# Two attentions of a two-layer network: strips gathered by DMAs of 48, 16 and 32 partitions, and the second attention's scores and sums taken by key blocks

## What is computed

```python
# first attention ("ratio")
q, k, v = split(LN(x) @ w_qkv + b_qkv)
dot     = q @ k.T                                     # per head, 512 x 512
scores  = dot * dot / (|q|^2 + |k|^2 - 2 * dot + 1e-6) # causal
x       = x + softmax(scores) @ v @ w_out + b_out
# second attention ("zeroed")
q, k, v = split(LN(x).reshape(heads) @ Wqkv + bqkv)
att     = (q @ k.T / 4) * tril(ones, k=-1)            # zeroed, not left out
x       = x + softmax(att) @ v @ Wr + br
```

## Time and profile before

| | |
|---|---|
| median of 3 runs | 2644.44 us |
| lowest, highest | 2637.9, 2645.82 us |
| the profiled execution | 2632.14 us |
| its span in the trace | 2630.4 us |
| TensorE matmul, busy | 2454.3 us (93%) |
| TensorE weight loads | 1750.0 us (67%) |
| VectorE | 2083.8 us (79%) |
| ScalarE | 1996.4 us (76%) |
| GpSimd | 1787.9 us (68%) |
| DMA, SP's and ScalarE's queues | 106176 packets and 175.82 MB; 3840 packets and 1.58 MB |

### The profile page before, as it was taken

One profiled execution on the slowest core, in us unless ns is written; L12 is line 12 of the kernel. 1 busy time (PEld: TensorE's weight loads), 2 busy tenths in 40 slices (PEclk: granted clock), 3 DMA queues, 4 the chain that ended last, 5 costly groups with the idle time before them and its releaser, 6 DMA issues. The chain is left out here.

```text
span 2630.4 us, 71983 instructions
## 1 busy us (share of the span) xinstructions
PE 2454.3 (93%) x25252; PEld 1750.0 (67%) x25252; DVE 2083.8 (79%) x6697; ACT 1996.4 (76%) x3679; POOL 1787.9 (68%) x3824
## 2 busy tenths in 40 slices
PE   5999999999999999999879989999999999989998
PEld 3677676667767666777423347767776777668887
DVE  5898898889889889988664578878888888846665
ACT  4999899999999999999524347677677666667776
POOL 4778778778877877887361137777777777756555
PEclk8999999999999999999989999999999999999999
DMA  4344244334334433433100146556655655400011
GB/s 119 65 74 81 55 73 85 72 61 83 72 58 79 85 71 61 77 69 63 37 6 1 37 74 111 99 101 98 106 101 95 105 104 94 64 1 32 25 33 41
DMA packets 110375, 182.00 MB, mean 69 GB/s; under 512 B 27008, under 2 KB 96384, under 8 KB 97920
## 3 DMA queue, kind: packets, MB, share of 16 engines
q1 hardware_dynamic: 106176, 175.82, 35.8%
q10 hardware_dynamic: 3840, 1.58, 0.4%
HBM read 116.25 MB, written 60.29 MB: 67 GB/s over the span
## 5 line engine op out<-in xcount | busy, mean ns | idle before, releaser
L921 POOL TENSOR_SCALAR ratio_scores<-ratio_scores,ratio_max_cols 128x512 f32<-128x512 f32 (+3 forms) x1024 | 539.3, 535 | 169.7 <-DVE ratio_max_cols L799 169.5
L205 PE MATMUL bank<-ratio_k_stack,ratio_q_stack 102*128 102x512 bf16 (+7 forms) x2048 | 508.7, 303 | 42.3 <-DVE ratio_max_cols L799 21.3
L1491 DVE CUSTOM_DVE_ANT_0 zeroed_unused<-bank,zeroed_drop 128x512 bf16<-128x512 f32 (+3 forms) x1024 | 439.7, 485 | 107.4 <-PE bank L205 107.2
L799 DVE CUSTOM_DVE_ANT_0 ratio_scores<-bank,ratio_scores 128x512 f32<-128x512 f32 (+3 forms) x1024 | 472.5, 490 | 22.2
L1373 ACT ACTIVATE arena<-bank 128x512 f32<-128x512 f32 x640 | 370.2, 593 | 151.0 <-PE bank L1266 149.6
L789 DVE TENSOR_TENSOR ratio_scores<-bank,ratio_inverse 128x512 f32<-128x512 f32 x640 | 435.6, 681 | 13.5 <-ACT ratio_inverse L648 6.5
L655 ACT ACTIVATE ratio_prob<-bank 128x512 f32<-128x512 f32 x640 | 378.6, 592 | 81.8 <-PE bank L554 80.9
L644 ACT ACTIVATE ratio_inverse<-bank 128x512 f32<-128x512 f32 x640 | 382.6, 598 | 13.4 <-PE bank L208 13.2
L554 PE MATMUL bank<-const_f_sb,ratio_scores 128*128 128x128 f32 x2560 | 386.5, 273 | 1.2 <-ACT ratio_prob L655 1.0
L648 ACT ACTIVATE ratio_inverse<-ratio_inverse 128x1024 f32<-128x1024 f32 x320 | 338.6, 1058 | 10.1
L1625 POOL TENSOR_SCALAR_AFFINE_SELECT arena<-arena 128x256 f32<-128x256 f32 (+1 forms) x640 | 228.0, 362 | 165.7 <-ACT arena L1373 161.2
(11 more groups left out here) (218 smaller groups left out, 4872.0 us busy)
## 6 DMA issues: line engine op xcount, KB each, us to landing
ratio_q_stack<-ratio_parts_q SPq DMA_DIRECT2D x186, 128.0 KB
ratio_k_stack<-ratio_parts_k SPq DMA_DIRECT2D x186, 128.0 KB
zeroed_q_stack<-zeroed_parts_q SPq DMA_DIRECT2D x186, 128.0 KB, 4.5
zeroed_k_stack<-zeroed_parts_k SPq DMA_DIRECT2D x186, 128.0 KB, 7.5
ratio_parts_q<-arena SPq DMA_DIRECT2D x96, 128.0 KB
ratio_parts_k<-arena SPq DMA_DIRECT2D x96, 128.0 KB
zeroed_parts_q<-shared_parts SPq DMA_DIRECT2D x96, 128.0 KB
zeroed_parts_k<-shared_parts SPq DMA_DIRECT2D x96, 128.0 KB
```

The lines of the kernel that those rows point to most:

```text
L205: i = e.matmul(bank[:, off:off + w], qs[0:rows, s, hh, ib * P:(ib + 1) * P], ks[0:rows, s, hh, 0:w], start=(k == 0), stop=mask is None, sk ...
L799: i = e.tensor_tensor_reduce(seg, dot_banks[n % 2][:, at], seg, 1.0, 0.0, ALU.mult, ALU.max, mx[:, pair % M_BUFS, c:c + 1])
L921: i = e.tensor_scalar(seg, seg, -1.0, mx[:, pair % M_BUFS, c:c + 1], ALU.mult, ALU.add)
L1491: i = e.tensor_tensor_reduce(unused[:, n % 2, at], bank[:, at], drop[:, L - (ib + 1) * P:L], 1.0, 0.0, ALU.add, ALU.max, mx[:, pair % FOLD ...
```

## The change

The k parts are stored in DRAM in reverse (part 2 first), the q parts as before. Then strips 0 to 2, strip 3 and strips 4 and 5 of both stacks are each a run of parts that lie next to each other in DRAM, and one DMA of 48, 16 or 32 partitions copies a run: six DMAs for a half instead of twelve. The six products of parts that a matmul sums are the same, in another order. The bytes are the same.

In the second attention `shift` no longer goes by query blocks. A unit now holds key blocks (`KEY_UNITS`: key block `jb = 3 - ib` with the queries from `jb` on, which has as many columns as query block `ib` had), one matmul for each segment. `attend_keys` sums in the order of key blocks 0, then 1 and 3, then 2, one matmul per head and key block over all queries from that block on, accumulating in the bank. `keep` picks the diagonal blocks at their new places: the first block of each segment.

The diff, without the two counts of semaphores in the first attention's `denoms` and the second's `dots`, which change in the same way as `gathered`:

```diff
-Q_PARTS = (0, 0, 1, 0, 2, 1)
-K_PARTS = (0, 1, 0, 2, 0, 1)
+STORED = ((0, 1, 2), (2, 1, 0))
+RUNS = ((0, 3, (0, 0)), (3, 1, (0, 2)), (4, 2, (0, 1)))
+GATHERS = 2 * len(RUNS)
+
+def gather_run(e, side, run, stack, dst, heads, stored):
+    strip, n, first = run
+    return e.dma_start(stack[strip * HD:(strip + n) * HD, dst, heads, :],
+                       stored[first[side]:first[side] + n, :, heads, :].rearrange("k d h t -> (k d) h t"))
...
-        gathered = lambda half: (s[f"gathered{half % 2}"], 16 * (14 * (half // 2 + 1) - 2 * (half % 2 == 0)))
+        gathered = lambda half: (s[f"gathered{half % 2}"], 16 * ((GATHERS + 2) * (half // 2 + 1) - 2 * (half % 2 == 0)))
...
-            for strip, part in enumerate((Q_PARTS, K_PARTS)[side]):
-                q.e.dma_start((qs, ks)[side][strip * HD:(strip + 1) * HD, st, heads, :],
-                              part_dram[side][st][part][:, heads, :]).then_inc(sem, 16)
+            for run in RUNS:
+                gather_run(q.e, side, run, (qs, ks)[side], st, heads, part_dram[side][st]).then_inc(sem, 16)
...
-                    e.dma_start(part_dram[side][half % 2][part].rearrange("d h t -> h d t"),
+                    e.dma_start(part_dram[side][half % 2][STORED[side][part]].rearrange("d h t -> h d t"),
                                 parts[:, side, part, :]).then_inc(s[f"parts_{sides[side]}"], 16)
...
+KEY_UNITS = [[(h, 3 - ib, off) for h, ib, off in segs] for segs in UNITS]
+WHERE_KEYS = {(h, jb): (u, off) for u, segs in enumerate(KEY_UNITS) for h, jb, off in segs}
+KEY_ATTEND = tuple(tuple(3 - ib for ib in blocks) for blocks in ATTEND)
...
-                first = True
-                for h, ib, off in UNITS[u]:
-                    wd, hh = (ib + 1) * P, (g % 2) * GROUP + h
-                    for jb in range(ib + 1):
-                        i = e.matmul(bank[:, off + jb * P:off + (jb + 1) * P], ks[0:STACK + FOLD_ROWS, st, hh, jb * P:(jb + 1) * P],
-                                     qs[0:STACK + FOLD_ROWS, st, hh, ib * P:(ib + 1) * P], start=first, stop=True, skip_group_check=True)
-                        first = False
+                for k, (h, jb, off) in enumerate(KEY_UNITS[u]):
+                    hh = (g % 2) * GROUP + h
+                    i = e.matmul(bank[:, off:off + L - jb * P], ks[0:STACK + FOLD_ROWS, st, hh, jb * P:(jb + 1) * P],
+                                 qs[0:STACK + FOLD_ROWS, st, hh, jb * P:L], start=(k == 0), stop=True, skip_group_check=True)
                 i.then_inc(s["shifted"])
+
+            def attend_keys(g, part):
+                vs, base = (g // 2) % STACKS, g * N_UNITS
+                for jb in KEY_ATTEND[part]:
+                    for h in range(GROUP):
+                        u, off = WHERE_KEYS[h, jb]
+                        i = e.matmul(o_bank[32 * h:32 * h + 32, jb * P:L], values_ones[:, vs, jb, (g % 2) * GROUP + h, :],
+                                     prob[:, (base + u) % FOLD_PROBS, off:off + L - jb * P],
+                                     start=(jb == 0), stop=(part == len(KEY_ATTEND) - 1), skip_group_check=True)
+                return i
...
-                    attend(e, g, part, o_bank, values_ones, prob, FOLD_PROBS, STACKS).then_inc(s["attended"])
+                    attend_keys(g, part).then_inc(s["attended"])
...
-                units = UNITS[n % N_UNITS]
+                units = KEY_UNITS[n % N_UNITS]
                 to = prob[:, n % FOLD_PROBS, :].rearrange("p (k t) -> p k t", k=T)
-                diagonal = to[:, 1::2, :] if len({ib for _, ib, _ in units}) < len(units) else to[:, T - len(units):T, :]
+                diagonal = to[:, 0:units[-1][2] // P + 1:max(units[-1][2] // P, 1), :]
```

More of the change, by code:

```diff
@@ L210, in product, with attend @@
     return i
-def attend(e, g, part, o_bank, values_ones, prob, bufs=PROB_BUFS, stacks=2):
-    vs, base = (g // 2) % stacks, g * N_UNITS
+def attend(e, g, part, o_bank, values_ones, prob):
+    vs, base = (g // 2) % 2, g * N_UNITS
     for ib in ATTEND[part]:
@@ L221, in attend @@
                              values_ones[:, vs, jb, (g % 2) * GROUP + h, :],
-                             prob[:, (base + u) % bufs, off + jb * P:off + (jb + 1) * P],
+                             prob[:, (base + u) % PROB_BUFS, off + jb * P:off + (jb + 1) * P],
                              start=(jb == 0), stop=(jb == ib), skip_group_check=True)
@@ L536, in denoms @@
             def denoms(n):
-                q.wait_ge(s["gathered_first"], 16 * 14)
+                q.wait_ge(s["gathered_first"], 16 * (GATHERS + 2))
                 if n >= N_UNITS:
@@ L1205, in zeroed_attention @@
         sides = "qk"
-        gathered = lambda half: (s[f"gathered{half % STACKS}"], 16 * 12 * (half // STACKS + 1))
+        gathered = lambda half: (s[f"gathered{half % STACKS}"], 16 * GATHERS * (half // STACKS + 1))
         folded = lambda pair: (s[f"m_folded{pair % 4}"], 16 * (pair // 4 + 1))
@@ L1250, in dots @@
             def dots(n):
-                q.wait_ge(s["gathered_first"], 16 * 12)
+                q.wait_ge(s["gathered_first"], 16 * GATHERS)
                 if n >= N_UNITS:
@@ L1682, in gather @@
                 q.wait_ge(s["shifted"], (half + 1 - STACKS) * HALF_UNITS)
-                for stack, side, order in ((qs, 0, Q_PARTS), (ks, 1, K_PARTS)):
-                    for strip, part in enumerate(order):
-                        e.dma_start(stack[strip * HD:(strip + 1) * HD, dst, heads, :],
-                                    part_dram[side][st][part][:, heads, :]).then_inc(sem, 16)
+                for stack, side in ((qs, 0), (ks, 1)):
+                    for run in RUNS:
+                        gather_run(e, side, run, stack, dst, heads, part_dram[side][st]).then_inc(sem, 16)
             for half in range(2, halves):
@@ L2141, in send_parts @@
                     for part in range(3):
-                        e.dma_start(start.part_dram[side][half][part].rearrange("d h t -> h d t"),
+                        e.dma_start(start.part_dram[side][half][STORED[side][part]].rearrange("d h t -> h d t"),
                                     start.parts[:, side, part, :]).then_inc(zs[f"parts_{sides[side]}"], 16)
@@ L2147, in gather @@
                 q.wait_ge(s["w_t"], 2)
-                for side, stack, parts in ((0, start.qs, Q_PARTS), (1, start.ks, K_PARTS)):
+                for side, stack in ((0, start.qs), (1, start.ks)):
                     q.wait_ge(zs[f"parts_{sides[side]}"], 48 * (half + 1))
-                    for strip, part in enumerate(parts):
-                        e.dma_start(stack[strip * HD:(strip + 1) * HD, half, heads, :],
-                                    start.part_dram[side][half][part][:, heads, :]).then_inc(sem, 16)
+                    for run in RUNS:
+                        gather_run(e, side, run, stack, half, heads, start.part_dram[side][half]).then_inc(sem, 16)
             send_parts(0)
```

## The result

Four executions of the changed kernel took 2616.32 to 2625.67 us, median 2617.66; four of the kernel before, 2637.9 to 2645.82, median 2643.11. The ratio is 0.9912, with a 95% interval from 0.9886 to 0.9938: 23 us faster, between 16 and 30. The forecast was 2626.6 us, 17.8 faster, in a range of 2613 to 2643. Run again beside its parts, the same kernel gave 0.9934 (0.9915 to 0.9954), 17 us. So it is faster by more than the 8 us that a measurement of this kernel can tell, and by about what was forecast; but not every term of the forecast's sum was right.

What follows compares the result with a forecast made beforehand. TensorE bounds the kernel: its DMA waits cost their whole length in the first attention, its own stream sets the second. Waits 16.3 plus start 1.5 make 17.8 us off 2644.4: 2626.6 us, 8 in 10 range 2613 to 2643.

Steps and rivals of the forecast that it cites:

- (a): Strip gathers, six DMAs per half instead of 12: rate rises from 161 to 240 GB/s, ending 3.3 us sooner.
- (b): SP's queue: three strip issues instead of six put the norms' send 1.4 us earlier; 0 if larger DMAs issue dearer.
- (c): First attention's boundaries: TensorE's waits for the norm rows all go, 16.3 us; bounds 0 and 16.3.
- (d): Start of the kernel: strips issued sooner, so TensorE's first product comes 1.5 us earlier; bounds 0 and 2.5 us.
- (e): `shift` in the second attention: 16 wide matmuls per group for 40 of 128 columns gain 0; rounding 6.4 us either way.
- (f): `attend_keys`: 16 wide matmuls per group for 40, four heads sharing the array, gain 0; rounding 2 us.
- (g): Second attention's strip gathers: issued two halves ahead, no `product` waits for them, so they gain 0.
- the rate rose: Against the rival that the gathers' rate does not rise: 0 to 3 us gained, about 2642 us; chance 0.14.
- no wait for the norms was left at the boundaries: Against the rival that uneven engine runs shrink the waits only in part, by 5 to 12 us: 2632 to 2639; chance 0.12.
- the wide tiles share the array: Against the rival that four wide column tiles in `attend_keys` do not run together: 138 us slower, 2765 us; chance 0.07.
- the narrow ones cost next to nothing: Against the rival that replacing narrow matmuls pays in the second attention: 64 us faster, 2563 us; chance 0.04.

Runs made afterwards that it cites:

- e6: The changed kernel, but in the first attention each of a half's six strip DMAs is cut into two of half the heads; ratio 0.9934 (0.9915 to 0.9953).
- the second kernel: The kernel before with shift, the sums and keep by key blocks alone, the 12 strips of 16 partitions kept; ratio 0.9984 (0.9969 to 1.0).

## Why the prediction was right, and where it was not

**(a) the rate:** right in direction, too high in size: 216 and 182 GB/s, not 240. The 161 GB/s that it started from are those of a later part of the gather; at the same place it was 180, so the 201 said to be needed were measured against too low a rate, too. The norm rows land 3.1 us sooner against the need (1.4 late, 1.7 early); forecast 3.3. But only 2.35 us of that is the gather (14.85 to 12.50 us from q's first issue); the other 0.8 is that it begins earlier before the need. That the size came out so well is in part luck. The Trainium skill (SBUF — State Buffer, Door 1: The DMA port swizzle) fits in direction and not in size: by its figures, an estimate, both stacks take 8.4 instead of 14.4 us, a rate 1.7 times higher. The windows rose by 20% and 34%.

**(b) the issues:** not dearer, as said. But the 1.4 us did not reach the norms' send: q's three issues end at 170.26, SP then stands, and the send goes at 171.29. From q's first issue to the second send (k's) it is 2.68 us, against 3.15 before: 0.5 us won. And e6 shows that the smaller number isn't needed for the gain.

**(c) the waits: the step that failed in part.** The forecast took all 16.3 us, on the ground that the odd halves "make up nothing". They do: before, each odd half after a wait was 0.42 us shorter than one after none. The evidence was in the trace of before: after the only even boundary with no wait, at 958.67, the next half took 38.80 us by the loads (to 997.47), not 38.33, but the rows shown ended at 958.67. What is late next is not TensorE's own stream: in the first units of the half VectorE's maxima hold up `dots`, and behind a late boundary, 9 us on, ScalarE holds up the projection; the difference between the two is the 0.42 us. The account: the 14 even boundaries that waited show 14.2 us over 37.63 (15.3 us of load waits), of which 13 give back 0.42, 5.5 us; boundary 1 gives 0.7; and a half-clock stretch behind the longest wait (264 us) added 1.45 (whether that wait caused it is open). Together 14.2 - 5.5 + 0.7 + 1.45 = 10.9 us, and the stage is 10.9 us shorter. So the term was 10.9 and not 16.3 us. It was also said that all 15 waits fall on even boundaries; one, of 0.97 us, is at the first.

**(d) the start:** 1.5 us taken; in nine profiles with k's and q's stack wide at the start the first `product` is at 36.15 to 37.15 us, mean 36.65, in two with both narrow at 37.3 and 38.3. That is 1.2 us, within the bounds; the 35.8 us that the prediction named were not reached.

**(e), (f) the wide matmuls:** forecast 0, with 0.01 us of rounding a unit or part; measured 0.20 us a row, 3.2 us in all, inside that rounding. The Trainium skill's price of 81 ns for a matmul of 128 columns (TensorE: Matmul & The Clock Gate, Back-to-back issue gap) is not borne out by the trace here either: by it (an estimate) four narrow ones would take 0.32 us and cost 0.1 us more than the wide one, which takes 0.22. The runs show that 24 fewer instructions of `shift` a group bring 0.12 us a row, four groups, hence 1.25 ns each. TensorE has 144 us less of weight loads, and no more than these 3.2 us came with it.

**(g)** held: 48.50 us a row with the gathers alone, 48.48 before.

**The rivals.** None came about: the rate rose, no wait for the norms was left at the boundaries, the wide tiles share the array (part 0 in 1.00 us), the narrow ones cost next to nothing.

**The sum.** 10.9 + 1.2 + 3.2 = 15.3 us can be shown, the whole run again says 17 and the two parts together 19, and the first measurement 23 (16 to 30). The total came near the forecast because a term too large by 5.4 us stood beside gains it had put at nothing: that is luck. What lies beyond 15 us is open. Executions of the kernel before vary by 16 us, and the time goes with the clock: among 37 of them, the correlation of the time with the time at the lower clock (reckoned from each one's mean granted clock) is 0.81. Its one profile waited 16.3 us for norms, that of the second kernel, with the same gathers, 19.4 us and was 3 us longer in that stage. Timed executions leave no trace, so whether longer waits there are the rest could not be shown.

## What to carry to other kernels

A wait's length is what it can cost at most, as long as the clock stays (two cases here suggest that it may fall behind a long wait, and none proves it). Compare the stretch behind a wait with the same stretch behind none, if the trace has one: what the next engine would have taken anyway comes off, here up to 0.42 us of each wait. And compare rates over windows that lie at the same place of the transfer. Where a transfer ends just too late, it is its rate when the engines are full that counts more than its issues, and of several transfers the one ahead of the late one in the queue.

## What the runs showed of the hardware that was not expected

At a full share of the 16 engines, gathers with 8 KB pieces moved 180 and 136 GB/s into 16 partitions a DMA, 216 and 182 with 48, 16 and 32, in windows at the same place of the gather; one issue of the wide kind cost SP 0.41 to 0.45 us in these gathers, one of the narrow kind 0.44 to 0.51. TensorE's clock in the last 16 us of the second attention's drain was 1.00 in some profiles and about 0.57 in others, and the drain took up to 4.3 us more where it fell. In the 10 us before the fall TensorE was busy 7.42 us, and as long in a kernel with the same drain where the clock stayed; what decides between the two was not found.
